# Moving the small routing tiles of a fused conv/MoE kernel into PSUM, and the normalisation of x from VectorE to ScalarE

## The chip, the cores and the metric

One Trainium2 chip, one core. The metric is the device time in microseconds (us) of the whole program, the median of three runs. The engines are called as the profile calls them: PE (TensorE), DVE (VectorE), ACT (ScalarE), POOL (GpSimd), SP (SyncE, which issues DMAs here).

## What is computed

A two-layer block on 16 images of 24 x 24 pixels and 128 channels (9216 tokens). Each layer normalises, convolves, adds, normalises again and then sends each token to 2 of 8 experts. Layer 0, from the reference, cut:

```
weight = codebook[_IDX] * _SIGNS                      # 7x7 depthwise
out = conv_general_dilated(x, weight, ..., feature_group_count=CHANNELS)
...
router_logits = einsum('bsd,de->bse', x, Wg)          # x: normalised over the 128 channels
top_logits, top_idx = top_k(router_logits, 2)
top_w = softmax(top_logits)
for e in range(8):
    out = out + cw[:, e:e+1] * (silu(xt @ W1[e]) @ W2[e])
```

Layer 1 is the same with an up/down-sampling convolution and a gated expert (`silu(x @ w1) * (x @ w3)`).

## The kernel before

The program is a row of stages, each with a block of code for every engine, and a barrier between them: `conv0_phase` (7x7 convolution on PE), `route0_phase` (first routing), `expert0_phase` (152 blocks of 128 rows through the experts), `conv1_expert1_phase` (second convolution, with the second routing run inside it, and then the second experts), and `combine_phase` (adds the answers and stores).

Routing works on 20 groups: 4 image groups `ig` times 5 pixel groups `q`. A group is 120 pixels (96 for q = 4) of 4 images, so a tile has 120 partitions and 4 x 128 channels. Per group, in the first routing:

- DVE `norm_measure` (L419, L422, L424): mean and variance of each row; `mv` holds them, `rstd` gets variance + eps.
- ACT `norm_root` (L431): square root of `rstd` in place. DVE `norm_scale` (L439): its reciprocal.
- DVE `route_dest` (L511) writes the 8 destinations of each row as integers into the payload `xn`, and `norm_apply` (L446, four instructions) writes the normalised x into `xn`.
- ACT `route_copy_rows` (L538) copies it for the second choice. PE turns it (L547), ACT copies the turned rows (L556), PE makes the logits (L566).
- DVE `route_pick` (L578 to L588): the two largest logits, their distance `gap`, flags `onehot` and `picked`, `group_sum`. ACT `route_exponent` (L596). PE `route_ranks` (L608 to L612) counts earlier tokens per expert.
- DVE `route_place` (L622 to L633): weights of the two choices, and `slot`, the row of the DRAM tensor `routed` for each of the 8 choices.
- POOL `route_scatter` (L645): 8 indirect DMAs that write `xn` to those rows.

`groups` writes out the five groups of image group 0 and loops over the other three. DVE's order in a step is: measure group g, pick g-1, scale and normalise g, place g-1. ACT's is: root g, exponent g-1, copy rows g, copy turned g. `Chain.after` makes DVE wait for the completion of its own instruction wherever the next one reads its result. `xn`, `slot` and their semaphores `scattered[q]` are rings of five groups, so DVE can be at most five groups ahead of POOL's scatters. The x tiles of group (ig, q) are loaded by SP (L864) once group (ig-1, q) is normalised; the first image group's loads are followed in SP's queue by eight large loads of weights and filter factors (L870, L397, L398). After the last group DVE also computes the table of expert blocks (L661 to L689) and four wide products and differences (L939, L942, L944, L946: filter factors and the low part of the expert weights `w1l`). The stage ends when every scatter has landed.

In the second routing the normalisation is already done by ACT (`norm_apply_by_act`, L463, with `shift` = -mean * rstd made by DVE at L454), and `route_dest` is a DVE step of its own in the convolution's hand-written order.

Of the kernel before, what the change touches and what calls it, by code (L numbers as in the profile page):

```python
# [28 lines left out]
P = 128  # L29
# [10 lines left out]
PAY = 132  # L40
# [323 lines left out]
class Routing:  # L364

    def __init__(self, nc, ctx):
        sb = lambda n, s, d=F32: ctx.enter_context(nc.sbuf_tensor(n, s, d))
        self.x = sb("x", [P, GROUPS, IG, P])
        self.ident = sb("ident", [P, P])  # L370

        self.before = sb("before", [P, P], BF16)
        self.ones = sb("ones", [P, P], BF16)
        self.blank = sb("blank", [P, EXPERTS, PAY])
        self.iota8 = sb("iota8", [P, CHOICES, EXPERTS])
# [25 lines left out]

class Norm:

    def __init__(self, nc, ctx, sem, name, eps):
        sb = lambda n, s: ctx.enter_context(nc.sbuf_tensor(f"{name}_{n}", s, F32))
        self.nc, self.eps = nc, eps
        self.stats, self.mv = sb("stats", [P, IG, 6]), sb("mv", [P, IG, 2])
        self.rstd, self.shift = sb("rstd", [P, IG]), sb("shift", [P, IG])
        self.chain, self.beat = sem(f"{name}_chain"), sem(f"{name}_beat")  # L410
        self.var_ready, self.std_ready, self.shifted, self.act_beat, self.applied = (sem(f"{name}_{n}") for n in ("var", "std", "shift", "act_beat", "applied"))

def norm_measure(m, dve, ig, q, x):

    nc, px, g = m.nc, pixels(q), QT * ig + q
    ch = Chain(dve, m.chain, NORM_STEPS * g)
# [6 lines left out]
    nc.vector.tensor_scalar(m.rstd[0:px], m.mv[0:px, :, 1], m.eps, None, ALU.add).then_inc(m.var_ready, 1)  # L424

def norm_root(m, act, ig, q):

    px = pixels(q)
    need(act, m.var_ready, QT * ig + q + 1)  # L430
    m.nc.scalar.activation(m.rstd[0:px], m.rstd[0:px], ACT.Sqrt).then_inc(m.std_ready, 1)  # L431

def norm_scale(m, dve, ig, q):

    nc, px, g = m.nc, pixels(q), QT * ig + q
    ch = Chain(dve, m.chain, NORM_STEPS * g + 2)
    need(dve, m.std_ready, g + 1)
    ch.after(nc.vector.reciprocal(m.rstd[0:px], m.rstd[0:px]))  # L439

def norm_apply(m, dve, ig, q, out, x):

    px = pixels(q)
# [3 lines left out]
    ins.then_inc(m.applied, 1)  # L448
# [19 lines left out]
class Router:  # L468

    def __init__(self, nc, ctx, sem, r, layer, xs, one_table=True):
# [3 lines left out]
        self.norm = Norm(nc, ctx, sem, f"ln{layer}", 1e-5)  # L475
        self.xn = sb("xn", [P, QT, 2, IG, PAY])
        self.xnt = sb("xnt", [P, IG, P])
        self.top, self.top_at = sb("top", [P, IG, 8]), sb("top_at", [P, IG, 8], U32)
        self.gap, self.ex, self.den = sb("gap", [P, IG]), sb("ex", [P, IG]), sb("den", [P, IG])
        self.onehot, self.picked = sb("onehot", [P, IG, 2, EXPERTS]), sb("picked", [P, IG, EXPERTS], BF16)  # L480
        self.earlier = sb("earlier", [P, EXPERTS], BF16)
        self.group_sum = sb("group_sum", [P, EXPERTS])
        self.rank, self.prod = sb("rank", [P, IG * EXPERTS]), sb("prod", [P, IG, 2, EXPERTS])
        self.slot_f, self.slot = sb("slot_f", [P, CHOICES]), sb("slot", [P, QT, CHOICES], I32)
# [20 lines left out]
def route_dest(ro, dve, ig, q):  # L505

    px = pixels(q)
    if isinstance(ig, int) and ig == 0 and q == 0:
        dve.wait_ge(ro.cleared, 2)
    need(dve, ro.scattered[q], 16 * CHOICES * ig)  # L510
    ro.nc.vector.tensor_copy(  # L511
        ro.xn[0:px, q, :, :, DEST].bitcast(I32),
        ro.r.dest[0:px, bass.ds(QT * ig + q, 1), :].rearrange("p a (t k) -> p k (a t)", k=2))

def route_normalise(ro, dve, ig, q):

    px = pixels(q)
    route_dest(ro, dve, ig, q)
    norm_apply(ro.norm, dve, ig, q, ro.xn[0:px, q, 0, :, 0:P],  # L520
                    ro.r.x[0:px, bass.ds(QT * ig + q, 1)].rearrange("p a t c -> p (a t) c"))

def route_normalise_by_act(ro, act, ig, q):
# [46 lines left out]
def route_pick(ro, dve, ig, q):  # L571
# [10 lines left out]
    nc.vector.tensor_tensor(ro.gap[0:px], ro.top[0:px, :, 1], ro.top[0:px, :, 0], ALU.subtract).then_inc(ro.gap_ready, 1)  # L582
# [3 lines left out]
    ch.after(nc.vector.tensor_tensor(ro.picked[0:px], ro.onehot[0:px, :, 0, :], ro.onehot[0:px, :, 1, :], ALU.add))  # L586
# [249 lines left out]
def route0_phase(nc, io, r, wt, xs, c0_x, x1d):  # L836

    with ExitStack() as ctx:
# [44 lines left out]
        def _(act):  # L883
# [39 lines left out]
        def _(dve):  # L923

            def step(ig, q):
# [6 lines left out]
                route_normalise(ro, dve, ig, q)  # L932
# [227 lines left out]
def experts_split(ex, dve, besides=None):  # L1160
    nc, U, layer, hid = ex.nc, ex.U, ex.layer, ex.hid

    def split(b, s, turn_no, early):
# [7 lines left out]
        nc.vector.tensor_copy(ex.dest[:, slot:slot + 1], ex.xg[:, slot, DEST:DEST + 1].bitcast(I32))  # L1171
# [98 lines left out]
def conv1_expert1_phase(nc, io, r, wt, xs, ys):  # L1270
# [8 lines left out]
    with ExitStack() as ctx:  # L1279
# [3 lines left out]
        lnc = Norm(nc, ctx, sem, "lnc", 1e-6)  # L1283
# [179 lines left out]
        def _(act):  # L1463
# [25 lines left out]
            def step(it, n):  # L1489
# [14 lines left out]
                for ig, q in due(it, n, after(3)):  # L1504
                    route_normalise_by_act(ro, act, ig, q)
# [11 lines left out]
        def _(dve):  # L1517
# [36 lines left out]
            def step(it, n):  # L1554
# [59 lines left out]
def host_layouts(a):  # L1614
# [44 lines left out]
    io["dest"] = (np.arange(GROUPS)[:, None] * TPX * CHOICES + p[:, None, None] * CHOICES + np.arange(CHOICES)).astype(np.int32)  # L1659
    blank = np.zeros((EXPERTS + SPARE, P, PAY), np.int32)  # L1660
    blank[:, :, DEST] = ANSWERS + np.arange((EXPERTS + SPARE) * P).reshape(EXPERTS + SPARE, P)
    io["blank"] = blank[:EXPERTS].transpose(1, 0, 2).reshape(P, EXPERTS * PAY).view(np.float32)
    io["blank_rows"] = blank[EXPERTS:].reshape(SPARE * P, PAY).view(np.float32)
# [57 lines left out]
```

## Time and profile before

| | us |
|---|---|
| median of the runs | 1527.68 (1527.48 to 1532.9, 3 runs) |
| profiled execution, span from first to last instruction | 1634.3 |
| first routing in that span, from POOL's first to its last scatter | 192.81 to 466.26 |

The profile gives the profiled execution by its span alone: 1634.3 us, 106.6 us (7.0%) above the median of the runs without a profile. Busy over the span: PE 1137.5 us (70%), DVE 976.8 (60%), POOL 735.5 (45%), ACT 641.0 (39%). The page cuts the span into 40 slices; the first routing is slices 5 to 12, in which PE is busy one or two tenths and its granted clock is 0.5 of full speed. A row of the timeline gives start, duration, engine, line, operation, tiles and, in brackets, how long the engine stood idle before it and what the profile takes for the releaser.

### The profile page before, as it was taken

Reading aid. Unit: us, or ns where it says so; the run is one execution under the profiler, and the core shown is the slowest. Engines: PE = TensorE matmul, PEld = TensorE weight load, DVE = VectorE, ACT = ScalarE, POOL = GpSimd, SP = SyncE. Lnnn points to the kernel's source line nnn. Section 1 sums busy time; section 2 is a strip of 40 time slices with the busy share of each in tenths; the row PEclk is TensorE's granted clock in tenths of the full one; section 3 lists DMA queues with packets and bytes.
Section 4 is the critical chain, followed back from the end, with each engine's and each line's share of the span. In section 5 each row is a group of like instructions: output and inputs, shape, how many; then the busy total and the mean of one; then the engine's idle time right before and its main releaser. Section 6 shows DMA issues by size and latency. Waiting matters only on the chain. (4 is left out here: it accounts for less than half of the span.)

```text
span 1634.3 us, 29161 instructions
## 1 busy us (share of the span) xinstructions
PE 1137.5 (70%) x6195; PEld 884.1 (54%) x6196; DVE 976.8 (60%) x3803; ACT 641.0 (39%) x1295; POOL 735.5 (45%) x703
## 2 busy tenths in 40 slices
PE   1697212222229999999848989899794699998930
PEld 0697212221229999998725555455452576777720
DVE  6664324443546666665465777668764677776744
ACT  2454223332314444444343655555554243343310
POOL 0332255556644444444351364574536555554420
PEclk9998555555559999999959999899896799999975
DMA  8242762221112222222150021221102222222249
GB/s 209 70 110 69 186 184 53 50 54 45 41 43 66 62 62 63 63 61 62 49 171 22 15 68 40 50 56 29 29 19 56 65 78 69 72 74 68 71 115 259
DMA packets 138877, 123.73 MB, mean 76 GB/s; under 512 B 65813, under 2 KB 119310, under 8 KB 137408
## 3 DMA queue, kind: packets, MB, share of 16 engines
q1 hardware_dynamic: 107149, 72.91, 18.6%
q0 software_dynamic: 19968, 39.44, 7.7%
q10 hardware_dynamic: 11667, 10.46, 2.3%
q14 instruction: 73, 0.60, 0.1%
q8 instruction: 20, 0.33, 0.1%
HBM read 72.74 MB, written 51.06 MB: 76 GB/s over the span
## 5 line engine op out<-in xcount | busy, mean ns | idle before, releaser
L645 POOL DMA_INDIRECT routed<-r_xn,r_slot x320 | 342.4, 1070 | 343.9 <-DVEq L634 219.9
L1020 POOL DMA_INDIRECT answers<-e_y,e_dest x152 | 146.0, 960 | 199.9 <-ACT e_y L1145 194.2
L1020 POOL DMA_INDIRECT answers<-c_c x152 | 146.1, 961 | 145.1 <-ACT c_c L1145 92.0
L1429 PE MATMUL c_pz<-c_c,down 116*120 116x512 f32 (+1 forms) x392 | 193.4, 610 | 0.0
L1197 DVE COPY e_ht<-e_ps_ht 128x512 f32<-128x512 f32 x152 | 105.2, 692 | 122.8 <-PE e_ps_ht L1066 120.1
L1076 PE MATMUL e_ps_y<-w,e_ht 128*128 x1216 | 160.8, 275 | 0.3 <-DVE e_ht L1197 0.3
L1076 PEld LDWEIGHTS e_ps_y<-w,e_ht 128*128 128x128 f32 x1216 | 147.8, 192 | 0.8 <-issue 0.6
L1403 PE MATMUL c_py<-c_xh,gl 121*116 121x512 f32 (+1 forms) x196 | 120.4, 614 | 35.9 <-DVE c_xl L1532 34.1
L1542 DVE SCALAR_TENSOR_TENSOR c_c<-c_a 116x1024 f32<-116x1024 f32 (+1 forms) x60 | 75.0, 1250 | 69.6 <-ACT c_a L1487 60.0
L608 PE MATMUL r_ps_rank<-r_picked,before 120*120 120x32 bf16 (+1 forms) x40 | 9.7, 243 | 151.7 <-DVEq L587 104.5
L1140 ACT ACTIVATE e_h<-e_ps_h 128x512 f32<-128x512 f32 x154 | 92.0, 597 | 58.3 <-PE e_ps_h L1056 56.1
L547 PE MATMUL r_ps_t<-ident,r_xn 120*128 120x120 f32 (+1 forms) x160 | 34.8, 361 | 107.7 <-DVE r_xn L446 44.4
L1197 DVE COPY c_c<-c_pz 128x256 f32<-128x256 f32 x152 | 64.3, 423 | 74.5 <-PE c_pz L1066 42.4
L1145 ACT ACTIVATE e_y<-e_ps_y,e_weight 128x128 f32<-128x128 f32 x152 | 56.0, 369 | 128.4 <-issue 100.5
L1487 ACT ACTIVATE c_a<-c_py 116x512 f32<-116x512 f32 x116 | 68.5, 590 | 95.6 <-PE c_py L1403 93.5
L1429 PEld LDWEIGHTS c_pz<-c_c,down 116*120 116x120 f32 (+1 forms) x392 | 68.7, 183 | 50.8 <-issue 42.5
L608 PEld LDWEIGHTS r_ps_rank<-r_picked,before 120*120 120x120 bf16 (+1 forms) x40 | 6.3, 158 | 158.0 <-DVEq L587 106.6
L1066 PE MATMUL e_ps_ht<-ident,e_h 128*128 128x128 f32 x608 | 91.2, 272 | 0.0
L547 PEld LDWEIGHTS r_ps_t<-ident,r_xn 120*128 120x128 f32 (+1 forms) x160 | 23.1, 189 | 125.7 <-DVE r_xn L446 45.8
L1066 PEld LDWEIGHTS e_ps_ht<-ident,e_h 128*128 128x128 f32 x608 | 75.3, 140 | 21.7 <-issue 0.6
L1136 ACT ACTIVATE c_c<-c_py 128x256 f32<-128x256 f32 x154 | 58.9, 383 | 62.4 <-PE c_py L1056 41.3
L1403 PE MATMUL c_py<-c_xl,gh 121*116 121x512 f32 (+1 forms) x196 | 81.9, 418 | 0.0
(206 smaller groups left out, 2999.9 us busy)
## 6 DMA issues: line engine op xcount, KB each, us to landing
answers<-answers SPq DMA_DIRECT2D x32, 480.0 KB
e_xg<-routed SPq DMA_DIRECT2D x159, 66.0 KB
c_c<-routed SPq DMA_DIRECT2D x159, 66.0 KB
c_w<-in_w SPq DMA_DIRECT2D x26, 393.8 KB
routed<-r_xn,r_slot POOLq DMA_INDIRECT x320
c_x<-in_xh SPq DMA_DIRECT2D x4, 1170.0 KB
w1l<-in_w SPq DMA_DIRECT2D x2, 2048.0 KB, 10.6
out<-x ACTq DMA_DIRECT2D x16, 240.0 KB
```

What stands on the lines that cost most here:

```text
L547: ins = ro.nc.tensor.transpose(ro.ps_t[:, t * P:t * P + px], ro.xn[0:px, q, 0, t, 0:P], ro.r.ident[0:px, 0:px])
L645: ro.nc.gpsimd.indirect_dma_start(ro.xs, bass.IndirectOffsetOnAxis(ap=ro.slot[0:px, q, c:c + 1], axis=0), ro.xn[0:px, q, k, t, :], None).t ...
L1020: ex.nc.gpsimd.indirect_dma_start(ex.ys, bass.IndirectOffsetOnAxis(ap=ex.dest[:, s:s + 1], axis=0), ex.y[:, s, :], None).then_inc(ex.store ...
L1066: ins = nc.tensor.transpose(ex.ps_ht[s % 2][:, c * P:(c + 1) * P], ex.h[:, s % 2, c * P:(c + 1) * P], r.ident[:])
L1076: ins = nc.tensor.matmul(ex.ps_y[s % 2][:, 0:P], ex.ht[:, s % 2, c * P:(c + 1) * P], wt.w2[:, bass.ds(w + c * P, P)], start=c == 0, stop=c ...
L1136: nc.scalar.activation(ex.gate[:, i, :], ex.ps_h[i][:, 0:ex.hid], ACT.Silu).then_inc(ex.gated, 1)
L1140: nc.scalar.activation(ex.h[:, i, :], ex.ps_h[i][:], ACT.Silu).then_inc(ex.hid_ready, 1)
L1197: nc.vector.tensor_copy(ex.ht[:, s % 2, :], ex.ps_ht[s % 2][:, 0:hid]).then_inc(ex.ht_ready, 1)
L1403: ins = nc.tensor.matmul(out, w[0:k, wcols], v, start=start and n == 0, stop=stop and n == 2)
L1429: ins = nc.tensor.matmul(ps_z[q % 3][0:rows, :], r.down[0:PPX, m * TPX:m * TPX + rows], c[0:PPX, p % R, :], start=p == ROWS * q, stop=p == ...
L1487: nc.scalar.activation(a[0:PPX, p // 2 % ARING, p % 2, :], ps_y[p % 2][0:PPX, :], ACT.Copy).then_inc(y_copied, 1)
L1542: nc.vector.scalar_tensor_tensor(out, raw, 0.2, raw, ALU.mult, ALU.max).then_inc(y_leaky, 1)
```

## The change

`Small` is a new helper: a room of 512 columns in one PSUM bank (or 256 columns of SBUF where `in_psum` is false), from which small tiles are cut. In the first routing it is in PSUM, three times: `norm` (`mv`, and a new `std` that holds variance + eps and its root, so that `rstd` is written only by the reciprocal), `dve` (`top_at`, `prod`, `group_sum`, `rank`, `slot_f`) and `weight` (`gap`, `ex`, `den`). In the second routing and the second convolution's norm it is in SBUF. `top`, `onehot`, `picked`, `earlier`, `rstd`, `shift`, `slot` stay in SBUF. `gap` is now made by four instructions with a per-partition scalar, `picked` by one reduction of `onehot`. `norm_apply` on DVE is gone: in both routings ACT applies the scale and shift, and `route_dest` is an ACT copy. For that, destinations are kept as float32 numbers (the constants too), and the experts' `dest` copy converts them to integers.

```diff
+class Small:
+    def __init__(self, nc, ctx, name, in_psum):
+        self.nc, self.ctx, self.name, self.in_psum = nc, ctx, name, in_psum
+    def of(self, user):
+        name = f"{self.name}_{user}"
+        room = self.ctx.enter_context(self.nc.psum_tensor(name, [P, 512], F32) if self.in_psum
+                                      else self.nc.sbuf_tensor(name, [P, 256], F32))
...
-        self.stats, self.mv = sb("stats", [P, IG, 6]), sb("mv", [P, IG, 2])
+        self.stats = sb("stats", [P, IG, 6])
+        self.mv, self.std = small(IG * 2).rearrange("p (t s) -> p t s", s=2), small(IG)
...
-    m.nc.scalar.activation(m.rstd[0:px], m.rstd[0:px], ACT.Sqrt).then_inc(m.std_ready, 1)
+    m.nc.scalar.activation(m.std[0:px], m.std[0:px], ACT.Sqrt).then_inc(m.std_ready, 1)
...
-    ch.after(nc.vector.reciprocal(m.rstd[0:px], m.rstd[0:px]))
+    ch.after(nc.vector.reciprocal(m.rstd[0:px], m.std[0:px]))
...
-def norm_apply(m, dve, ig, q, out, x):
-    for t in range(IG):
-        ins = m.nc.vector.tensor_scalar(out[:, t, :], x[:, t, :], m.mv[0:px, t, 0:1], m.rstd[0:px, t:t + 1],
-                                           ALU.subtract, ALU.mult)
...
+        self.top, self.top_at = sb("top", [P, IG, 8]), eights().bitcast(U32)
+        self.gap, self.ex, self.den = weight(IG), weight(IG), weight(IG)
+        self.onehot, self.prod = sb("onehot", [P, IG, 2, EXPERTS]), pairs()
+        self.picked, self.earlier = sb("picked", [P, IG, EXPERTS], BF16), sb("earlier", [P, EXPERTS], BF16)
+        self.group_sum, self.rank, self.slot_f = own(EXPERTS), own(IG * EXPERTS), own(CHOICES)
...
-def route_dest(ro, dve, ig, q):
+def route_dest(ro, act, ig, q):
-    ro.nc.vector.tensor_copy(
-        ro.xn[0:px, q, :, :, DEST].bitcast(I32),
+    ro.nc.scalar.activation(
+        ro.xn[0:px, q, :, :, DEST],
         ro.r.dest[0:px, bass.ds(QT * ig + q, 1), :].rearrange("p a (t k) -> p k (a t)", k=2), ACT.Copy)
...
-    nc.vector.tensor_tensor(ro.gap[0:px], ro.top[0:px, :, 1], ro.top[0:px, :, 0], ALU.subtract).then_inc(ro.gap_ready, 1)
+    for t in range(IG):
+        less = nc.vector.tensor_scalar(ro.gap[0:px, t:t + 1], ro.top[0:px, t, 1:2], ro.top[0:px, t, 0:1], None, ALU.subtract)
+    less.then_inc(ro.gap_ready, 1)
...
-    ch.after(nc.vector.tensor_tensor(ro.picked[0:px], ro.onehot[0:px, :, 0, :], ro.onehot[0:px, :, 1, :], ALU.add))
+    with nc.allow_low_precision(reason="a sum of two flags is 0 or 1"):
+        flags = nc.vector.tensor_reduce(ro.picked[0:px], ro.onehot[0:px].rearrange("p t k e -> p t e k"), AX.X, ALU.add)
+    ch.after(flags)
...
                 norm_root(ro.norm, act, ig, q)
+                route_dest(ro, act, ig, q)
                 if last:
                     route_exponent(ro, act, *last)
+                route_normalise(ro, act, ig, q)
                 route_copy_rows(ro, act, ig, q)
...
                 norm_scale(ro.norm, dve, ig, q)
-                route_normalise(ro, dve, ig, q)
+                norm_shift(ro.norm, dve, ig, q)
...
-        nc.vector.tensor_copy(ex.dest[:, slot:slot + 1], ex.xg[:, slot, DEST:DEST + 1].bitcast(I32))
+        nc.vector.tensor_copy(ex.dest[:, slot:slot + 1], ex.xg[:, slot, DEST:DEST + 1])
```

How this moves DVE's instructions in the first routing. Before, in the step of group (0, 1), from `gap` of group (0, 0) on:

```order
L582 TENSOR_TENSOR r_gap<-r_top 120x4
L584 TENSOR_TENSOR r_onehot<-iota,r_top_at 120x64 [waits c0_cleared]
L586 TENSOR_TENSOR r_picked<-r_onehot 120x32 [waits c0_cleared]
L588 TENSOR_REDUCE r_group_sum<-r_picked 120x8 [waits c0_cleared]
L439 RECIPROCAL ln_rstd<-ln_rstd 120x4 [waits c0_blank_in]
L511 COPY r_xn<-dest 120x8 [waits c0_mean_w_in]
L446 TENSOR_SCALAR r_xn<-x,ln_mv,ln_rstd 120x128 x4
L622 TENSOR_SCALAR r_den<-r_ex 120x4 [waits c0_var_eps]
L625 TENSOR_TENSOR r_earlier<-r_earlier,r_group_sum 120x8 [waits c0_cleared,c0_std]
L626 TENSOR_TENSOR r_rank<-r_ps_rank,region 120x32
```

The same place after the change (`r_small_...` are the cuts of the PSUM rooms; the names behind "waits" are those of semaphores used again from an earlier stage):

```order
L586 TENSOR_SCALAR r_small_weight<-r_top 120x1 x4
L589 TENSOR_TENSOR r_onehot<-iota,r_small_dve 120x64 [waits c0_cleared]
L592 TENSOR_REDUCE r_picked<-r_onehot 120x32 [waits c0_cleared]
L595 TENSOR_REDUCE r_small_dve<-r_picked 120x8 [waits c0_cleared]
L459 RECIPROCAL ln_rstd<-r_small_norm 120x4 [waits c0_blank_in]
L465 SCALAR_TENSOR_TENSOR ln_shift<-r_small_norm,ln_rstd 120x4 [waits c0_mean_w_in]
L629 TENSOR_SCALAR r_small_weight<-r_small_weight 120x4 [waits c0_var_eps]
L632 TENSOR_TENSOR r_earlier<-r_earlier,r_small_dve 120x8 [waits c0_cleared,c0_std]
L633 TENSOR_TENSOR r_small_dve<-r_ps_rank,region 120x32
```

The destination copy and the four 120x128 instructions are gone from between the reciprocal and the place part; one 120x4 instruction stands there. On ACT, from the start of group (0, 0) into group (0, 1), before:

```order
L431 ACTIVATE ln_rstd<-ln_rstd 120x4 [waits c0_route_consts]
L538 ACTIVATE r_xn<-r_xn 120x4x128 [waits c0_x_in2]
L556 ACTIVATE r_xnt<-r_ps_t 128x4x120 [waits c0_mean]
L431 ACTIVATE ln_rstd<-ln_rstd 120x4 [waits c0_route_consts]
L596 ACT_TABLE_LOAD
L596 ACTIVATE r_ex<-r_gap 120x4 [waits c0_var]
L538 ACTIVATE r_xn<-r_xn 120x4x128 [waits c0_x_in2]
L556 ACTIVATE r_xnt<-r_ps_t 128x4x120 [waits c0_squared,c0_mean]
L431 ACT_TABLE_LOAD
```

And after:

```order
L451 ACTIVATE r_small_norm<-r_small_norm 120x4 [waits c0_route_consts]
L525 ACTIVATE r_xn<-dest 120x8 [waits c0_w_free]
L474 ACTIVATE r_xn<-x,ln_shift,ln_rstd 120x128 [waits c0_x_in0]
L474 ACTIVATE r_xn<-x,ln_shift,ln_rstd 120x128 x3
L541 ACTIVATE r_xn<-r_xn 120x4x128 [waits c0_x_in2]
L559 ACTIVATE r_xnt<-r_ps_t 128x4x120 [waits c0_mean]
L451 ACTIVATE r_small_norm<-r_small_norm 120x4 [waits c0_route_consts]
L525 ACTIVATE r_xn<-dest 120x8
L603 ACT_TABLE_LOAD
L603 ACTIVATE r_small_weight<-r_small_weight 120x4 [waits c0_var]
L474 ACTIVATE r_xn<-x,ln_shift,ln_rstd 120x128 [waits c0_x_in0]
L474 ACTIVATE r_xn<-x,ln_shift,ln_rstd 120x128 x3
```

ACT has five instructions more per group: the destination copy behind the root, and four of scale and shift behind the exponent, ahead of the two copies of rows (L541, L559).

## Rows read from the trace of the kernel before

**Rows 1.** Busy time by stretch; columns as the first row names them

```profile
core 0: us, PE busy (x) PEld busy (x) DVE busy (x) ACT busy (x) POOL busy (x), PEclk, DMA share, GB/s
...
190.00:467.00 277.00, 64.59 (x324) 53.90 (x324) 123.23 (x767) 81.25 (x113) 165.85 (x160) 0.50 0.32 77
...
850.00:1265.00 415.00, 352.32 (x1301) 208.94 (x1301) 280.79 (x1099) 214.17 (x422) 210.46 (x181) 0.92 0.15 40
```

**Rows 2.** Waits, stretch 190 to 467 us: who waited for whom, total, times, longest

```profile
POOL routed L645 <- issue: 78.9, 149, 32.4
POOL routed L645 <- DVEq L634: 61.2, 11, 11.8
```

**Rows 3.** Timeline of POOL, first routing: start, length, tiles, idle before

```profile
192.81 1.18 POOL L645 DMA_INDIRECT routed<-r_xn,r_slot  x1 [32.42 <-issue]
...
250.14 0.93 POOL L645 DMA_INDIRECT routed<-r_xn,r_slot  x1 [11.76 <-DVEq L634]
...
292.08 1.00 POOL L645 DMA_INDIRECT routed<-r_xn,r_slot  x1 [7.45 <-DVEq L634]
...
301.19 0.99 POOL L645 DMA_INDIRECT routed<-r_xn,r_slot  x1 [0.30 <-issue]
...
465.34 0.92 POOL L645 DMA_INDIRECT routed<-r_xn,r_slot  x1 [0.30 <-issue]
```

**Rows 4.** Waits of DVE, stretch 190 to 470 us

```profile
DVE r_top L578 <- remote: 31.4, 5, 7.3
DVE r_xn L627 <- remote: 27.1, 5, 6.3
DVE r_onehot L584 <- remote: 22.0, 5, 6.2
```

**Rows 5.** Timeline of DVE and ACT, 298 to 305 us

```profile
298.50 0.15 DVE L625 TENSOR_TENSOR r_earlier<-r_earlier,r_group_sum 120x8 bf16<-120x8 bf16 x1
298.57 0.18 DVE L626 TENSOR_TENSOR r_rank<-r_ps_rank,region 120x32 f32<-120x32 f32 x1
...
301.40 0.63 ACT L538 ACTIVATE r_xn<-r_xn 96x512 f32<-96x512 f32 x1 [6.17 <-DMA c_x<-in_xh]
...
304.50 0.18 DVE L627 RECIPROCAL r_xn<-r_den 120x4 f32<-120x4 f32 x1 [5.75 <-remote]
```

**Rows 6.** Timeline of DVE, 429 to 435 us

```profile
431.08 0.19 DVE L586 TENSOR_TENSOR r_picked<-r_onehot 120x32 bf16<-120x32 f32 x1 [1.20 <-issue]
432.62 0.21 DVE L588 TENSOR_REDUCE r_group_sum<-r_picked 120x8 f32<-120x32 bf16 x1 [1.35 <-DVE r_picked L586]
432.75 0.17 DVE L439 RECIPROCAL ln_rstd<-ln_rstd 96x4 f32<-96x4 f32 x1
434.06 0.17 DVE L511 COPY r_xn<-dest 96x8 int32 x1 [1.14 <-DVE ln_rstd L439]
```

**Rows 7.** Timeline of DVE, 410 to 420 us: one step without a long gap

```profile
412.65 0.87 DVE L419 BATCH_NORM_STATS2 ln_stats<-x 120x6 f32 x4 [0.37 <-DVE r_slot L633]
...
419.82 0.29 DVE L419 BATCH_NORM_STATS2 ln_stats<-x 96x6 f32 x1 [0.37 <-issue]
```

**Rows 8.** Groups by line, DVE from 190 to 467 us: busy, mean ns

```profile
L446 DVE TENSOR_SCALAR r_xn<-x,ln_mv,ln_rstd 120x128 f32 (+3 forms) x75 | 20.9, 348 | 0.0
...
L626 DVE TENSOR_TENSOR r_rank<-r_ps_rank,region 120x32 f32<-120x32 f32 (+1 forms) x20 | 3.6, 181 | 0.0
...
L625 DVE TENSOR_TENSOR r_earlier<-r_earlier,r_group_sum 120x8 bf16<-120x8 bf16 (+1 forms) x20 | 3.3, 166 | 0.0
```

**Rows 9.** The lines of ACT's scale and shift: min/median/max ns

```profile
L463 ACT ACTIVATE r_xn<-x,ln_shift,ln_rstd x80: 477/478/494, 896.6 to 1246.7; 120x128 f32<-120x128 f32 x32, 120x128 f32 x32, 96x128 f32 x8, 96x128 f32<-96x128 f32 x8
```

**Rows 10.** Timeline of POOL and DVE, 456 to 464 us

```profile
456.22 7.59 POOL L645 DMA_INDIRECT routed<-r_xn,r_slot  x1 [0.30 <-issue]
456.85 1.83 DVE L944 TENSOR_TENSOR gl<-factor_a,gh 128x1624 fp32r<-128x1624 f32 x1
458.61 4.41 DVE L946 TENSOR_TENSOR w1l<-w1l,w1h 128x4096 fp32r<-128x4096 f32 x1
```

More of the change, by code:

```diff
@@ L377, in __init__ @@
         self.block_no = sb("block_no", [1, TABLE])
-        self.dest = sb("dest", [P, GROUPS, CHOICES], I32)
+        self.dest = sb("dest", [P, GROUPS, CHOICES])
         self.wg = sb("wg", [P, 2, EXPERTS])
@@ L399, in weights_load, with cut, __init__ @@
                   io[f"w2_{layer}"].rearrange("p e c d -> p e (c d)")).then_inc(w_in, 16)
+class Small:
[5 more added lines that the diff above has]
+                                      else self.nc.sbuf_tensor(name, [P, 256], F32))
+        at = [0]
+        def cut(cols):
+            at[0] += cols
+            return room[:, at[0] - cols:at[0]]
+        return cut
 class Norm:
-    def __init__(self, nc, ctx, sem, name, eps):
+    def __init__(self, nc, ctx, sem, name, eps, small):
+        small = small.of("norm")
         sb = lambda n, s: ctx.enter_context(nc.sbuf_tensor(f"{name}_{n}", s, F32))
         self.nc, self.eps = nc, eps
-        self.stats, self.mv = sb("stats", [P, IG, 6]), sb("mv", [P, IG, 2])
+        self.stats = sb("stats", [P, IG, 6])
+        self.mv, self.std = small(IG * 2).rearrange("p (t s) -> p t s", s=2), small(IG)
         self.rstd, self.shift = sb("rstd", [P, IG]), sb("shift", [P, IG])
@@ L474, in __init__ @@
         self.nc, self.r, self.layer, self.xs = nc, r, layer, xs
-        self.norm = Norm(nc, ctx, sem, f"ln{layer}", 1e-5)
+        small = Small(nc, ctx, f"r{layer}_small", one_table)
+        self.norm = Norm(nc, ctx, sem, f"ln{layer}", 1e-5, small)
+        own, weight = small.of("dve"), small.of("weight")
         self.xn = sb("xn", [P, QT, 2, IG, PAY])
         self.xnt = sb("xnt", [P, IG, P])
[L478 to L484, printed above, removed]
+        eights = lambda: own(IG * 8).rearrange("p (t e) -> p t e", e=8)
+        pairs = lambda: own(CHOICES * EXPERTS).rearrange("p (t k e) -> p t k e", k=2, e=EXPERTS)
+        self.top, self.top_at = sb("top", [P, IG, 8]), eights().bitcast(U32)
[3 more added lines that the diff above has]
+        self.group_sum, self.rank, self.slot_f = own(EXPERTS), own(IG * EXPERTS), own(CHOICES)
+        self.slot = sb("slot", [P, QT, CHOICES], I32)
         self.count, self.tail_i = sb("count", [P, EXPERTS]), sb("tail_i", [1, EXPERTS], I32)
@@ L502, in route_clear @@
     ro.nc.gpsimd.memset(ro.earlier[:], 0.0).then_inc(ro.cleared, 1)
-def route_dest(ro, dve, ig, q):
[L507 to L510, printed above, removed]
-    ro.nc.vector.tensor_copy(
-        ro.xn[0:px, q, :, :, DEST].bitcast(I32),
[L513 to L524, printed above, removed]
+def route_dest(ro, act, ig, q):
     px = pixels(q)
@@ L529, in route_normalise_by_act, with route_normalise @@
     need(act, ro.scattered[q], 16 * CHOICES * ig)
+    ro.nc.scalar.activation(
+        ro.xn[0:px, q, :, :, DEST],
+        ro.r.dest[0:px, bass.ds(QT * ig + q, 1), :].rearrange("p a (t k) -> p k (a t)", k=2), ACT.Copy)
+def route_normalise(ro, act, ig, q):
+    px = pixels(q)
     norm_apply_by_act(ro.norm, act, ig, q, ro.xn[0:px, q, 0, :, 0:P],
@@ L1504, in step @@
                 for ig, q in due(it, n, after(3)):
-                    route_normalise_by_act(ro, act, ig, q)
+                    route_dest(ro, act, ig, q)
+                    route_normalise(ro, act, ig, q)
                 for ig, q in due(it, n, after(8)):
@@ L1657, in host_layouts @@
     io["block_no"] = np.arange(TABLE, dtype=f32).reshape(1, TABLE)
-    io["dest"] = (np.arange(GROUPS)[:, None] * TPX * CHOICES + p[:, None, None] * CHOICES + np.arange(CHOICES)).astype(np.int32)
-    blank = np.zeros((EXPERTS + SPARE, P, PAY), np.int32)
+    io["dest"] = (np.arange(GROUPS)[:, None] * TPX * CHOICES + p[:, None, None] * CHOICES + np.arange(CHOICES)).astype(f32)
+    blank = np.zeros((EXPERTS + SPARE, P, PAY), f32)
     blank[:, :, DEST] = ANSWERS + np.arange((EXPERTS + SPARE) * P).reshape(EXPERTS + SPARE, P)
-    io["blank"] = blank[:EXPERTS].transpose(1, 0, 2).reshape(P, EXPERTS * PAY).view(np.float32)
-    io["blank_rows"] = blank[EXPERTS:].reshape(SPARE * P, PAY).view(np.float32)
+    io["blank"] = blank[:EXPERTS].transpose(1, 0, 2).reshape(P, EXPERTS * PAY)
+    io["blank_rows"] = blank[EXPERTS:].reshape(SPARE * P, PAY)
     fu, fd = np.asarray(a["L1_conv_up_filter"]), np.asarray(a["L1_conv_down_filter"])
```

7 lines of the change are left out of this document (2 added, 5 removed).

## The prediction

> **What bounds the kernel now.** I read first the busy time by stretch, then who waits in the stretch that the change touches, then the timeline there. In the 277 us of the first routing no engine is full: POOL 165.9 us, DVE 123.2, ACT 81.3, PE 64.6 [rows 1]. The stage cannot end before POOL's last scatter has landed, so POOL's row is the one to read. It issues 160 scatters from 192.81 to 466.26 us, 273.5 us. Inside a run of scatters they follow each other at (301.19 - 292.08) / 7 = 1.30 us, so a group of eight costs POOL 10.4 us and 20 groups 208 us [rows 3]. The rest is waiting and a late obstruction. Waiting: 11 times POOL stood still for a slot that DVE had not written (DVEq L634), 61.2 us in all, 11.76 at most; less the 0.30 us that lie between any two scatters this is 61.2 - 3.3 = 57.9 us [rows 2, 3]. The 32.4 us in the other row of that view is the time ahead of the first scatter, and no gap between groups. Obstruction: one scatter takes 7.59 us, while DVE runs L944 and L946, two wide instructions with both inputs in SBUF [rows 10]; that is 6.6 us over its usual 1.0. So 208 + 57.9 + about 7 is the stage.
>
> Is DVE too slow for POOL? Not by its work: a step that meets no long gap takes 419.82 - 412.65 = 7.17 us, three microseconds less than POOL needs for a group [rows 7]. It is slow by gaps: 31.4 us ahead of L578, 27.1 ahead of L627, 22.0 ahead of L584, five times each, up to 7.3 us [rows 4]. The profile has no engine as their releaser. They lie in POOL's runs, and two stretches tell what they are. At 298.5 DVE has just finished L446; ACT, which waits for exactly that, goes on only at 301.40, and DVE itself gets no further than L626 until 304.50, when POOL's run (last scatter at 301.19) has drained [rows 3, 5]. And from 431 to 434 three short instructions in a row are held for 1.20, 1.35 and 1.14 us, each about one pitch of a scatter [rows 6]. I read this as DVE instructions that must wait for something that POOL holds while it makes a scatter. The scatter of 7.59 us is the same thing the other way round.
>
> **The change, part by part**, in the time of the profiled execution.
>
> *Instructions that can collide.* Per group the change takes out of the first routing every DVE instruction with two SBUF inputs (L582, L586, L625, L630 and L584, L629 get one operand in PSUM or become another instruction) and the SBUF-to-SBUF copy and scalar operations (L424, L446, L511, L622, L633). What the gaps stand behind in rows 5 and 6 is L625, L586 and L439, two of them with two SBUF inputs. What stays SBUF to SBUF is the statistics (L419), the maximum's output and the reduction for `picked`. Upper end of the gain: all 57.9 us of POOL's waiting [rows 2]. Lower end: nothing, if what stays is held in the same way. I take nearly all, because DVE has slack: even if 1.5 us per group of holding is left, DVE's step stays under 10.4 us, and it may run up to five groups ahead. I leave out the longest gap's half, 5 us (11.76 us at 250.14, rows 3), because it lies behind the bulk loads of weights and of x for the second image group, which the change doesn't touch. Gain: 57.9 - 5 = 53 us.
>
> Here a rule can be weighed. Rows 6 show one hold behind a reciprocal with a single SBUF input (L439, 1.14 us), which speaks for a remainder. By the Trainium skill ("SBUF — State Buffer", section "Who interferes with whom") a VectorE instruction with at most one SBUF input and outside the 2-port modes does not contend with GpSimd at all. By that rule the sum would be the full 57.9 us; by the rows alone some of it stays.
>
> *ACT instead of DVE on x.* DVE loses 20.9 / 75 x 4 = 1.11 us per group (L446, rows 8) and ACT gets four instructions of 478 ns [rows 9], at most 1.91 us. They lie in the loop shift, scale x, turn, logits, pick, reciprocal, so a step gets 0.8 us longer. The three additional instructions for `gap` cost at most 3 x 0.15 = 0.45 us, estimated by L625's 166 ns. Reading PSUM: L626, which has one PSUM input, takes 181 ns against 166 for L625, so ten such instructions cost 0.15 us more [rows 8]. The destination copy on ACT adds at most 0.2 us. Together 7.17 + 0.8 + 0.45 + 0.15 + 0.2 = 8.8 us per step. POOL's 10.4 us hide all of it; if POOL did not cover it, it would cost 1.6 x 20 = 32 us. ACT's busy time rises from 81 to about 81 + 20 x 2.1 = 123 us of 277, or of the 220 that should be left, so it does not become the bound.
>
> *First slot.* The step of group 1 must end before POOL starts. Its own L446 no longer lies ahead of the place part (-1.1 us), group 0's scale on ACT is 0.8 us longer: nothing.
>
> *End of the stage.* After the last slot DVE has the table and the four wide instructions, some 20 us, which still hold POOL up by about 7 us [rows 10]. With DVE ahead by several groups they lie under POOL's remaining scatters. That 7 us is in both kernels, so it drops out.
>
> *Second routing.* There ACT gets the destination copy (20 times 0.2 us), DVE loses it and gets three small instructions; small tiles stay in SBUF. PE is busy 352.3 of 415 us there, DVE 280.8, ACT 214.2 [rows 1]. I cost it at nothing, with PE as cover; without it, 20 x 0.3 = 6 us. The float destinations cost the experts nothing: one copy of one element becomes one conversion of one element.
>
> Sum: 1634.3 - 53 = 1581 us of span. The runs without profile are 7.0% shorter (1527.7 / 1634.3 = 0.935), and where those 107 us lie the profile doesn't say. I scale: 53 x 0.935 = 50, so 1527.7 - 50 = **1477 us**. The extremes of this case: all 57.9 us and a little from the second routing, 1527.7 - 63 = 1464; or gaps that are a third smaller without the profiler, 1527.7 - 33 = 1495.
>
> **The rivals.**
>
> *A: half of the gaps stay.* Statistics and other one-input instructions are held as L439 was [rows 6]; POOL waits for half of its 57.9 us. Gain 29 x 0.935 = 27: 1501 us. For it: rows 6, and gaps ahead of L578 that stand behind L424 and the statistics. Against it: a step has 1.6 us of slack.
>
> *B: the change doesn't do what it says.* The gaps come from something else in the stage, say completions that are reported late while DMAs run, or they exist mainly under the profiler. Then POOL goes on waiting, and only the small costs and savings remain: 1520 to 1535, 1528 us. For it: the releaser of the long gaps is "remote", and the gaps ahead of L578 stand ahead of an instruction that reads PSUM. Against it: the gaps' lengths in scatters, and the lengthened scatter of rows 10.
>
> *C: slower.* The gaps stay, and the loop, which is then what POOL waits for, is longer by its 1.6 us per step, since a slot is made one round of the loop later. Place: DVE's wait for the logits after ACT's scale. It decides from the point where held steps average over 10.4 us, as they do now (273.5 / 20 = 13.7). Price 1.6 x 20 x 0.935 = 30 us: 1558 us. 
>
> **How the numbers follow.** Forecast 0.61, A 0.19, B 0.12, C 0.08. About 0.5% (8 us) is what a measurement of this kernel can tell from no change. Faster is the forecast and A, 0.80; within 0.5% is B, 0.12; slower is C, 0.08. The range reaches from 1464 to 1524: it holds the forecast and A and leaves out C, nearly all of B and a few in a hundred below. Case by case that is 0.79 inside.
>
> **What would show it.** In the trace after: POOL's waits for the slot under 10 us instead of 61.2; its 160 scatters within about 220 us; the "remote" gaps of DVE gone; ACT's four scale instructions of about 0.48 us per group; the step of DVE paced by the ring (waits for `scattered`) in the later groups; the convolution stage as long as before. Wrong would be: gaps of several microseconds on DVE inside POOL's runs (A or B), or POOL still waiting for DVE with ACT's scale ahead of it (C). If the gaps are gone and the stage is not shorter, the pitch of 1.30 us must have grown.

## The result and the profile after

The changed kernel takes 1534.78 us (median of 20 runs, 1529.5 to 1540.23) against 1531.0 us for the kernel before in the same comparison (20 runs). The ratio is 1.0028, 95% interval [1.0016, 1.0041]: 4 us slower where 50 us faster was forecast, and outside the range. One run of the kernel before took 2114.7 us, and of its 80 runs in the later comparisons one took 4000.19 us; neither is in a ratio or has a trace, and the other 19 here lie between 1525.34 and 1536.46.

The page of the profile after, its head and busy time (us, share of the span, instructions):

```profile
span 1535.0 us, 29364 instructions
## 1 busy us (share of the span) xinstructions
PE 1124.8 (73%) x6195; PEld 880.8 (57%) x6196; DVE 970.5 (63%) x3823; ACT 681.8 (44%) x1415; POOL 735.0 (48%) x703
```

This execution took 1537.13 us, 2.1 us more than its span, and lies among the other 19 runs (1529.5 to 1540.23). So profiling as such does not cost 100 us, and the record that the prediction read, with a span of 1634.3 us, was not "the kernel under the profiler" but one execution that was about 105 us longer than the ordinary ones. The kernel before was therefore profiled again, unchanged (first experiment below). Its span is 1526.8 us, and all comparisons from here on are with that record.

Who waits, stretch 190 to 467 us, in the profile after (total, times, longest, in us):

```profile
POOL routed L652 <- issue: 46.9, 154, 0.3
...
POOL routed L652 <- ACT r_xn L541: 33.0, 2, 32.7
POOL routed L652 <- DVEq L641: 0.9, 3, 0.3
...
DVE r_top L581 <- PE r_ps_l L569: 35.3, 16, 3.4
```

The same views of the kernel before, profiled again:

```profile
POOL routed L645 <- issue: 79.3, 155, 32.4
...
POOL routed L645 <- DVEq L634: 0.9, 3, 0.3
...
DVE r_xn L511 <- DMA routed<-r_xn,r_slot: 13.7, 5, 3.4
...
DVE r_top L578 <- PE r_ps_l L566: 9.4, 16, 1.9
```

POOL's 61.2 us of waiting for the slot [rows 2] are 0.9 us in both: three of the 0.3 us that lie between any two scatters. In this record, POOL never waits for DVE once it has started. There was nothing for the change to remove. DVE instead waits for POOL (13.7 us, for landed scatters: it is its five groups ahead). The "remote" rows of DVE [rows 4] are absent.

First and last scatter and the lengthened one, timeline of POOL and DVE, the kernel before again and then after:

```profile
193.57 1.18 POOL L645 DMA_INDIRECT routed<-r_xn,r_slot  x1 [32.41 <-issue]
...
370.91 7.37 POOL L645 DMA_INDIRECT routed<-r_xn,r_slot  x1 [0.30 <-issue]
371.24 1.83 DVE L944 TENSOR_TENSOR gl<-factor_a,gh 128x1624 fp32r<-128x1624 f32 x1
373.00 4.41 DVE L946 TENSOR_TENSOR w1l<-w1l,w1h 128x4096 fp32r<-128x4096 f32 x1
...
406.62 0.92 POOL L645 DMA_INDIRECT routed<-r_xn,r_slot  x1 [0.30 <-issue]
```

```profile
194.09 1.18 POOL L652 DMA_INDIRECT routed<-r_xn,r_slot  x1 [32.67 <-ACT r_xn L541]
...
374.15 7.37 POOL L652 DMA_INDIRECT routed<-r_xn,r_slot  x1 [0.30 <-issue]
...
407.35 0.92 POOL L652 DMA_INDIRECT routed<-r_xn,r_slot  x1 [0.30 <-issue]
```

Both routings last 214 us. A scatter of 120 rows starts every 1.30 us (about 1.00 busy, 0.30 between), one of 96 rows, as the last one, every 1.23. What is left is five lengthened scatters near the end. Four of them are 2.36, 1.28, 1.42 and 1.10 us long (2.26, 1.28, 1.42, 1.10 after) and one 7.37 us, in place of 1.0: 8.5 us over in the one kernel, 8.4 in the other. Two of the five stand beside the table of blocks, and the timeline of DVE and POOL there (the kernel before again) shows what lengthens them:

```profile
361.23 1.48 DVE L671 TENSOR_TENSOR r_passed<-block_no,r_upto 1x1280 f32<-1x1280 f32 x1
362.30 1.28 POOL L645 DMA_INDIRECT routed<-r_xn,r_slot  x1 [0.30 <-issue]
362.74 1.48 DVE L673 TENSOR_REDUCE r_tab<-r_passed 1x160 f32<-1x1280 f32 x1
363.88 0.99 POOL L645 DMA_INDIRECT routed<-r_xn,r_slot  x1 [0.30 <-issue]
364.25 1.48 DVE L674 TENSOR_TENSOR r_passed<-r_passed,r_nblk 1x1280 f32<-1x1280 f32 x1
365.18 1.42 POOL L645 DMA_INDIRECT routed<-r_xn,r_slot  x1 [0.31 <-issue]
365.76 1.47 DVE L675 TENSOR_REDUCE r_tab<-r_passed 1x160 f32<-1x1280 f32 x1
366.91 0.99 POOL L645 DMA_INDIRECT routed<-r_xn,r_slot  x1 [0.30 <-issue]
```

All four scatters begin while a DVE instruction of 1.5 us runs. The two beside an instruction with two SBUF inputs (L671, L674) end 0.87 us after it (363.58 against 362.71, 366.60 against 365.73); the two beside a reduction with one input keep their 0.99 us. The scatter of 7.37 us ends 0.87 us after L946 too (378.28 against 377.41).

The stages by POOL's scatters in the timelines, first start to last start (the first routing to the last one's end), in us:

| | first routing | first experts | second routing | second experts | end of DVE's last |
|---|---|---|---|---|---|
| before, the long record | 273.4 | 324.0 | 357.4 | 286.1 | 1624.2 |
| before, again | 214.0 | 322.9 | 353.1 | 248.8 | 1516.9 |
| before, a third time | 214.5 | 322.9 | 355.1 | 248.2 | 1519.4 |
| after | 214.2 | 322.9 | 357.4 | 248.0 | 1524.4 |

Of the 107 us by which the long record is longer, 59.4 lie in the first routing and 37.3 in the second experts. Busy time is nearly the same in both records of before (DVE 976.8 and 977.4 us, POOL 735.5 and 731.2), so on these engines the 107 us are idle time.

### The profile page after: what moved, and what is told of

It reads as the page before. It is cut to its first block and busy times, and to the rows that moved or that the text cites. A ratio compares the mean times of both kernels' runs of the same rounds, so it can differ in the third digit from the quotient of the medians.

```text
span 1535.0 us, 29364 instructions
## 1 busy us (share of the span) xinstructions
PE 1124.8 (73%) x6195; PEld 880.8 (57%) x6196; DVE 970.5 (63%) x3823; ACT 681.8 (44%) x1415; POOL 735.0 (48%) x703
## 5 line engine op out<-in xcount | busy, mean ns | idle before, releaser
L1438 PE MATMUL c_pz<-c_c,down 116*120 116x512 f32 (+1 forms) x392 | 197.3, 620 | 0.0
L1054 PE MATMUL e_ps_x<-ident,e_xg 128*128 128x128 f32 x155 | 42.9, 277 | 58.5 <-DMA e_xg<-routed 58.5
L200 POOL TENSOR_TENSOR c_nrm<-c_cen,c_rstd 120x384 f32<-120x384 f32 x26 | 34.0, 1312 | 103.4 <-DVE c_pl L319 54.0
L474 ACT ACTIVATE r_xn<-x,ln_shift,ln_rstd 120x128 f32 (+3 forms) x160 | 65.8, 481 | 39.5 <-DVE ln_shift L465 39.3
```

Of the source, the lines that this page charges most:

```text
L474: ins = m.nc.scalar.activation(out[:, t, :], x[:, t, :], ACT.Identity, bias=m.shift[0:px, t:t + 1], scale=m.rstd[0:px, t:t + 1])
L1438: ins = nc.tensor.matmul(ps_z[q % 3][0:rows, :], r.down[0:PPX, m * TPX:m * TPX + rows], c[0:PPX, p % R, :], start=p == ROWS * q, stop=p == ...
```

## The experiments

Ratios are to runs of the kernel before on the same chip. Theory after the result: POOL bounds the first routing in the ordinary execution (160 scatters at 1.30 us), DVE's gaps belong to the long record, and two SBUF inputs matter only where a DVE instruction is long. Rival, the prediction's own: small DVE instructions and POOL hold each other up.

**The kernel before again** (no edit).

> The kernel before, profiled again. Theory T1 (the profiled execution of before was an unusually long one; ordinarily POOL scatters without gaps already): span about 1530 us, POOL's waits for the slot (DVEq L634) under 10 us in the first routing, no gaps of 3 us or more on DVE there, the stage from first to last scatter about 208 + 7 = 215 us. Rival T2 (the gaps are ordinary, and the change gave its gain back elsewhere): 50 to 60 us of such waits, stage about 273 us. Rival T3: something between, 10 to 50 us.

Measured: 1528.37 us, 0.9987 [0.9968, 1.0007], span 1526.8, shown above. DVE still has gaps of over 3 us (3.4 for landed scatters, 3.8 and 8.7 ahead of the statistics L419), against the expectation, but POOL feels none of them. The place of rows 5 in this record, timeline of all engines:

```profile
297.74 1.11 DVE L446 TENSOR_SCALAR r_xn<-x,ln_mv,ln_rstd 96x128 f32 x4
298.76 0.16 DVE L622 TENSOR_SCALAR r_den<-r_ex 120x4 f32<-120x4 f32 x1
298.83 0.16 DVE L625 TENSOR_TENSOR r_earlier<-r_earlier,r_group_sum 120x8 bf16<-120x8 bf16 x1
298.88 0.63 ACT L538 ACTIVATE r_xn<-r_xn 96x512 f32<-96x512 f32 x1 [3.80 <-DVE r_xn L446]
298.90 0.90 PE L547 MATMUL r_ps_t<-ident,r_xn 96*128 96x96 f32 x4 [2.84 <-DVE r_xn L446]
298.91 0.18 DVE L626 TENSOR_TENSOR r_rank<-r_ps_rank,region 120x32 f32<-120x32 f32 x1
299.07 0.99 POOL L645 DMA_INDIRECT routed<-r_xn,r_slot  x1 [0.30 <-issue]
299.13 0.18 DVE L627 RECIPROCAL r_xn<-r_den 120x4 f32<-120x4 f32 x1
```

ACT and PE start the moment L446 ends, in the middle of a run of scatters, with L625 (two SBUF inputs) beside them. In the long record [rows 5] L446 had ended at about 298.5, and ACT went on at 301.40; the same record has PE and SP there too:

```profile
301.39 0.60 SPq L864 DMA_DIRECT2D x<-x  x1
301.40 0.63 ACT L538 ACTIVATE r_xn<-r_xn 96x512 f32<-96x512 f32 x1 [6.17 <-DMA c_x<-in_xh]
301.42 0.90 PE L547 MATMUL r_ps_t<-ident,r_xn 96*128 96x96 f32 x4 [4.78 <-DMA c_x<-in_xh]
```

Three engines start together 2.9 us late, 0.2 us after POOL's last scatter of the run began. In the kernel all three wait for one semaphore that L446 sets (`applied`); the DMA that the rows name as releaser is nothing that they wait for. DVE's own instructions were not slower. So what came late, as this record has it, was the word of their completion; why is not known.

**After, with DVE scaling x and writing the destinations in the first routing**, PSUM tiles kept.

```diff
-                norm_shift(ro.norm, dve, ig, q)
+                route_dest_dve(ro, dve, ig, q)
+                norm_apply(ro.norm, dve, ig, q, ...)
```

> The changed kernel with x scaled and destinations written by DVE in the first routing, so of the change there only the PSUM tiles stay. T1: POOL is the bound in any case, so within 3 us of the kernel before; if ACT's scale is what makes the first slot later, 1 to 2 us faster than the changed kernel. T2: DVE's gaps come back at L-lines of the scale, stage 20 us or more longer.

Measured: 1531.59 us, 1.0002 [0.9986, 1.0019]; first slot at 193.37, first routing 213.2 us.

**After, with the small tiles in SBUF.**

```diff
-        small = Small(nc, ctx, f"r{layer}_small", one_table)
+        small = Small(nc, ctx, f"r{layer}_small", False)
```

> The changed kernel with the small tiles of the first routing in SBUF; ACT still scales x. T1: within 3 us of the kernel before, POOL without gaps. T2: instructions with two SBUF inputs are held in POOL's runs, waits for the slot 20 us or more and the time 15 us or more above the changed kernel.

Measured: 1535.28 us, 1.0022 [1.0007, 1.0038]; first routing 214.1 us, POOL waits 1.8 us for slots. Where the tiles lie makes no difference that these runs can tell; a step of DVE that nothing holds takes 8.2 us in both.

**After, with the second routing as before** (destinations by DVE, two-input forms of `gap` and `picked` there).

```diff
+    if ro.layer:
+        less = nc.vector.tensor_tensor(ro.gap[0:px], ro.top[0:px, :, 1], ro.top[0:px, :, 0], ALU.subtract)
...
+                    route_dest_dve(ro, dve, ig, q)
```

> The changed kernel with the second routing as before (destinations by DVE, gap and picked by tensor_tensor). If the 4 us by which the changed kernel is slower come from the second routing, this is 3 to 4 us faster than it, equal to before; if they come from the first routing, it stays 3 to 5 us above before.

Measured: 1530.97 us, 1.0004 [0.9987, 1.0021]; second routing 354.9 us.

**Both undone, only the PSUM tiles and the split instructions of the first routing kept.**

> The kernel after with both other parts undone: in both routings VectorE writes the destinations, in the first it also applies scale and shift, and the second routing has the two tensor_tensor forms of before. What stays are the PSUM tiles and the split instructions of the first routing. If the few microseconds by which the kernel after is slower come from the moved work (either routing), this is at 1.000 of the kernel before, 1529 to 1532. If the PSUM tiles cost them, it is at 1.002 to 1.003, about 1535.

Measured: 1531.28 us, 1.0005 [0.9991, 1.0018]. With the run that has the tiles in SBUF (1.0022) this points to the moved work and not to the PSUM tiles as what costs the 4 us. How they split between the two routings stays open: each part undone alone brings nearly all of them back, within intervals of about 2.5 us on either side, and the second routing of two records of the same kernel differs by 2.0 us.

**Three additional DVE instructions per group with two SBUF inputs** (x + x, 120 x 512), in the kernel before.

```diff
+                for n in range(3):
+                    nc.vector.tensor_tensor(probe[0:px, n, :], r.x[...], r.x[...], ALU.add)
```

> The kernel before, with three additional VectorE instructions per group at the end of its step in the first routing, each x + x over 120x512, both inputs in SBUF. By their size about 0.7 us each, 2.1 per group, 42 us in all; VectorE's step would be 7.2 + 2.1 = 9.3 us, still under the 10.4 us that POOL needs for the eight scatters of a group, so their own time is hidden. The prediction's mechanism (VectorE and POOL hold each other up wherever a VectorE instruction has two SBUF inputs): scatters are lengthened as the one of 7.4 us beside the wide products was, so the routing grows from 214 us by up to 42 us, and the time goes to 1545 to 1570. Rival (small and medium instructions hardly meet POOL, and only the last wide ones do): the routing stays 214 to 220 us and the time 1531 to 1537.

**The same with one SBUF input.**

```diff
-                    nc.vector.tensor_tensor(probe[0:px, n, :], r.x[...], r.x[...], ALU.add)
+                    nc.vector.tensor_tensor(probe[0:px, n, :], r.x[...], ps_j[0:px, :], ALU.add)
```

> The same with x + a PSUM tile of zeros, so that each of the three additional instructions has one SBUF input. By the prediction's mechanism nothing is held: the first routing stays 214 us, the time 1530 to 1534, while the kernel with two SBUF inputs is longer. By the rival both cost the same, under 6 us. If both are long by the same amount, it is VectorE's own time that counts, and neither's ports.

Measured: 1534.45 us, 1.0017 [0.9999, 1.0034] with two; 1531.27 us, 0.9996 [0.9981, 1.0012] with one. The first routing is 218.5 us with two and 214.2 with one. Timeline of both, first the kernel with two:

```profile
285.02 1.89 DVE L939 TENSOR_TENSOR probe_out<-x 120x512 f32 x3 [0.16 <-DVE r_slot L633]
285.19 1.38 POOL L645 DMA_INDIRECT routed<-r_xn,r_slot  x1 [0.30 <-issue]
```

```profile
285.96 0.99 POOL L645 DMA_INDIRECT routed<-r_xn,r_slot  x1 [0.30 <-issue]
286.65 1.88 DVE L940 TENSOR_TENSOR probe_out<-x,probe_ps 120x512 f32<-120x512 f32 x3 [0.16 <-DVE r_slot L633]
287.25 0.93 POOL L645 DMA_INDIRECT routed<-r_xn,r_slot  x1 [0.30 <-issue]
```

With two SBUF inputs the scatter that begins beside them takes 1.38 us in place of 1.0; with one it takes 0.93, the usual length for 96 rows. Twelve more scatters than usual are over 1.08 us (1.21 to 1.45), and POOL's busy time in them is 169.9 against 165.6 us: the 4.3 us by which the stage is longer. DVE's own instruction is nearly the same length in both, 687 and 682 ns:

```profile
L939 DVE TENSOR_TENSOR probe_out<-x 120x512 f32 x36 | 22.8, 687 | 1.9 <-DVE r_slot L633 1.3 <-issue 0.2
```

```profile
L940 DVE TENSOR_TENSOR probe_out<-x,probe_ps 120x512 f32<-120x512 f32 x45 | 28.2, 682 | 2.3 <-DVE r_slot L633 1.3 <-issue 0.2
```

So the collision exists, but it is POOL that is held and not DVE, and it costs 4.3 / 60 = 0.07 us on average for an instruction of 120 x 512. The difference is that of the two traces' stages; the runs' ratios alone (their intervals overlap) would not show it. By the Trainium skill ("SBUF — State Buffer", section "Who interferes with whom") a VectorE instruction with two SBUF inputs contends with a GpSimd instruction that reads SBUF, and one with at most one SBUF input, outside the 2-port modes, does not; the pair of runs agrees, 218.5 against 214.2 us. The run with one input shows a second thing: 60 additional instructions, 41 us of DVE's time, cost nothing. That is DVE's slack under POOL.

**The wide instructions fed through PSUM**, in the kernel before. ACT copies one input of L939, L942, L944 and L946 into one of four PSUM banks, in chunks of at most 512 columns, and DVE works chunk by chunk; ACT's copy of `gh` goes ahead of that of `w1h`.

```diff
-            nc.vector.tensor_tensor(wt.w1l[:], wt.w1f, wt.w1h[:].bitcast(F32), ALU.subtract)
+            use(lambda c, v: nc.vector.tensor_tensor(wt.w1l[:, c], wt.w1f[:, c], v, ALU.subtract), chunks(8, 512))
...
+            stage(wt.w1h[:].bitcast(F32), chunks(8, 512))
```

> The kernel before, with the four wide two-input VectorE instructions at the end of the first routing (products of the filter factors, low parts of the factors and of the expert weights) cut in chunks of at most 512 columns, one input of each chunk copied by ScalarE into one of four PSUM banks. What the numbers of small tiles did not show, the wide ones should: two profiles have scatters of 2.3, 1.3, 1.4, 1.1 and 7.4 us there in place of 1.0, 8.6 us together, in a stretch in which POOL is never waiting. If two SBUF inputs are the cause, all scatters are 1.0 us, the first routing takes 205 to 207 us in place of 214, and the time is 1521 to 1525. If it is any wide VectorE instruction, the lengthened scatters stay (spread over more of them) and the time stays 1528 to 1533.

Measured: 1524.06 us (1519.82 to 1526.08), 0.9941 [0.9918, 0.9963]; first routing 207.1 us. Timeline of the place where the scatter of 7.37 us was:

```profile
374.24 4.85 DVE L971 TENSOR_TENSOR w1l<-w1l,r_wide 128x512 fp32r<-128x512 f32 x8
374.44 1.00 POOL L645 DMA_INDIRECT routed<-r_xn,r_slot  x1 [0.30 <-issue]
375.74 1.00 POOL L645 DMA_INDIRECT routed<-r_xn,r_slot  x1 [0.30 <-issue]
377.04 0.99 POOL L645 DMA_INDIRECT routed<-r_xn,r_slot  x1 [0.30 <-issue]
378.34 0.99 POOL L645 DMA_INDIRECT routed<-r_xn,r_slot  x1 [0.31 <-issue]
```

Four scatters pass beside the same difference, at their usual length. Only three scatters of this kernel's stage, after the first, are still long (1.77, 1.42, 1.10: 1.3 us over in place of 8.5), where all were expected at 1.0: 1.77 and 1.42 stand beside L671 and L674, which the edit leaves with two SBUF inputs. The 7.2 us less are the stage's 6.9 and the program's 7. The edit does two things, it cuts the instructions and it moves one input. That two inputs lengthen a scatter is shown by the table's rows and by the pair of 120 x 512 runs. How much cutting alone would have brought is not shown: beside the uncut x + x instructions of 512 columns, three in a row, a scatter takes 1.45 us at most, so it may be a good part of the 7 us; against that, the scatter of 7.37 us began beside L942 (1.39 us from 369.93) and was let go at the end of neither L942 nor L944.

**The changed kernel with the same edit**, two banks.

> The kernel after with the wide instructions at the end of the first routing cut and fed through PSUM as in the run of the kernel before with that edit (here two banks, since the small tiles hold three). If the gain there (7 us, 0.994) is that of the lengthened scatters and the change's 4 us are separate from it, they add: 1527 to 1529, 0.997. If the two banks make ScalarE and VectorE alternate so slowly that the table is late, the second stage starts later and the time is above 1530.

Measured: 1526.67 us, 0.9977 [0.9963, 0.9992]; first routing 206.7 us. The two effects add, within the intervals.

**The PSUM tiles without the moved work, with the same edit.**

> The small PSUM tiles of the first routing without the moved work, together with the wide instructions fed through PSUM: no VectorE instruction after the first group has two SBUF inputs. If small tiles in PSUM bring anything beside the wide ones, this is below the 1524 of the kernel before with the wide edit alone; if, as the runs so far say, they bring nothing, it is 1522 to 1526, ratio 0.993 to 0.997.

Measured: 1525.03 us, 0.9962 [0.9948, 0.9976]; first routing 206.6 us. The small tiles bring nothing that shows beside the wide ones. The best version is the kernel before with the wide edit alone, or this one; both beat the two kernels of the case.

**The kernel before a third time** (no edit).

> The kernel before, profiled a third time. If its long profile (span 1634.3) is a frequent kind of execution, a third look shows it again, or spreads between; if it is a rare one, the span is 1525 to 1531, the first routing 213 to 215 us with POOL waiting under 2 us for slots, and the second experts 247 to 250 us.

Measured: span 1529.4 us, first routing 214.5 us, and again no wait of POOL for a late slot (1.5 us are five usual distances):

```profile
POOL routed L645 <- DVEq L634: 1.5, 5, 0.3
```

None of the twelve records made after the long one is like it. What makes an execution long was not found, nor whether the two long runs without a trace (2114.7 and 4000.19 us) have to do with it. Its other piece, the second experts, shows the same kind of wait, 1283 to 1570 us, first in the long record, then in the second:

```profile
POOL answers L1020 <- ACT c_c L1145: 92.0, 49, 4.2
...
PE c_pz L1066 <- DVE c_c L1183: 19.0, 22, 3.5
```

```profile
POOL answers L1020 <- ACT c_c L1145: 26.2, 24, 3.1
```

## Why the prediction was wrong

**The step that failed** is the one from the profile to the runs. The prediction took 57.9 us of POOL's waiting from the 1634.3-us record and multiplied by 0.935, saying that the profile does not tell where the other 107 us lie. Measured: the 57.9 us are 0 in an ordinary execution, so the gain was 0 and not 53 x 0.935 = 50. The gaps that the change was credited with removing were more than half of the excess itself. A uniform factor was not right: as the second record shows, durations of instructions are the same in the long and the short one (a scatter about 1.0 us, pitch 1.30 us, busy time within 0.6% on DVE and POOL), so the excess of 107 us is idle time, and idle time is where the forecast took its gain. The numbers at hand allowed the other sum: 160 x 1.30 + 7 = 215 us for the stage without gaps, which is what every ordinary record shows (214.0 to 214.5 for both kernels).

**The mechanism.** "DVE instructions that must wait for something that POOL holds" was read from rows 5 and 6. With an excess of idle time in the record, three holds of about a pitch were no evidence for a port. In ordinary records DVE's small instructions run through POOL's scatters without such holds, and longer ones with two SBUF inputs lengthen the scatter instead: 120 x 512 by 0.07 us each on average, 1 x 1280 (L671, L674) by 0.3 and 0.4 us, the pair L944 and L946 by 6.4 us. So "the same thing the other way round" was only half right: POOL is held, DVE is not. It matters most in the one place that the prediction saw [rows 10] and then let drop out, "in both kernels". That it is in both kernels was right (7.37 us in each), and the 7 us there are the only gain that these runs found: the wide edit gets them.

**What held.** DVE has slack under POOL's 10.4 us per group: 41 us of additional work cost nothing, and the ACT detour was covered as forecast. A step of DVE was costed at 7.17 + 1.6 = 8.8 us. From one reciprocal to the next, where nothing holds the step, DVE's timeline has 7.2 us before (the kernel before again) and 8.2 after:

```profile
233.56 0.17 DVE L439 RECIPROCAL ln_rstd<-ln_rstd 120x4 f32<-120x4 f32 x1
240.72 0.17 DVE L439 RECIPROCAL ln_rstd<-ln_rstd 120x4 f32<-120x4 f32 x1
```

```profile
226.19 0.17 DVE L459 RECIPROCAL ln_rstd<-r_small_norm 120x4 f32<-120x4 f32 x1
234.43 0.17 DVE L459 RECIPROCAL ln_rstd<-r_small_norm 120x4 f32<-120x4 f32 x1
```

So it grew by 1.1 us and not by 1.6. From the end of the reciprocal to the end of the logits it is 4.8 us before and 5.5 after in the first groups, 0.7 more where 0.8 was forecast for ACT's scale (481 ns per instruction, 478 forecast; the destination copy is 212 ns, 0.2 forecast). DVE's wait for the logits rose by more, from 9.4 to 35.3 us over 16 times, because DVE, rid of L446 and the copy, also comes to it earlier. The 0.15 us for reading PSUM had no ground: L626 and L625, whose 181 and 166 ns it was taken from, differ in width (32 and 8 columns) too, and the step is 8.2 us with the tiles in PSUM as in SBUF. The 0.65 us that the prediction names beside them is not seen either. The first slot was costed at nothing; from DVE's first statistics to the first scatter it is 12.8 us after and 12.5 before, 0.3 us later, and 12.9 in the two runs with DVE's scale and the tiles in PSUM (1.0002 and 1.0005), which are not slower than the kernel before. The second routing was costed at nothing, with 6 us as the uncovered price; undoing it brings the ratio from 1.0028 to 1.0004, so a part of the 4 us may lie there, though the first routing's part undone gives as much.

**The rivals.** B had the number, 1520 to 1535, with the words "or they exist mainly under the profiler". It was right that the gaps were of the record and not of the kernel, and wrong in blaming the profiler: twelve later records under it have spans of 1521 to 1535 us. Its other reason, completions that are reported late, is what the long record shows at 298.5 to 301.40; that it is while DMAs run is not shown. Its number goes by the small costs, 1528; the 4 us of those that came have no settled place. It had 0.12 and was nearly left out of a range that stopped at 1524. With a record 7% above every run shown, and the whole gain made of gaps in that record, it should have been the first case. A did not come: not half of the gaps stay, but none exist. C needs steps of over 10.4 us; the step grew by 1.1 us to 8.2, and POOL never waited for it.

## What to carry to other kernels

Before any wait of a profile is priced, hold the span against the timed runs: if it is longer by more than their spread, the excess may sit in the very waits that are to be priced (here 59.4 of 107 us did), so take another record or build the stage from durations and pitch (scatters x pitch) and price only what that sum leaves. An engine that issues scatters back to back can be the bound of a stage though it is busy for only half of the program; look for the instructions beside which one of its scatters is long. Cutting VectorE instructions over a thousand columns wide that overlap such scatters, and moving one of their two SBUF inputs to PSUM, was worth 7 us in four instructions; on small ones moving an input brought nothing. Whether the cut alone would do is the run to make next.

## What the runs showed of the hardware that was not expected

One execution was about 105 us longer than its fellows, with DVE and POOL busy for no longer. In one place of it three engines that wait for one DVE instruction start together 2.9 us after its end, at the last scatter of POOL's run. A DVE difference of 128 x 4096 with both inputs in SBUF, with the one ahead of it, holds one scatter for 7.37 us; cut in eight, with one input in PSUM, it lets scatters of 1.00 us pass and takes 4.85 us in place of 4.41. A scatter that begins beside L671 or L674, two SBUF inputs of 1280 columns on one partition, ends 0.87 us after it; beside a reduction of the same length with one input it keeps its 0.99 us. DVE instructions of 120 x 512 with two SBUF inputs lengthen twelve scatters from about 1.0 to 1.21 to 1.45 us and are not slower themselves (687 against 682 ns).
